# The first key projection between TensorE's turns, and three of eight one-hots multiplied on GpSimd

## What is computed

```python
xn = _layernorm(x, axis=-1)
# s: attention
q = (xn @ Wq + bq)                      # 8 heads of 128
k, v = split(xn @ Wkv + bkv)            # one head of 128 each
q, k = q + pe, k + pe                   # sinusoidal positions
probs = softmax(causal(q k^T / sqrt(128)))
s = (probs @ v) @ Wo
# g: experts, two of eight for each token
logits = xn @ router_w + router_b
gating = softmax(logits, the two largest kept)
y_e = relu(xn @ w1[e] + b1[e]) @ w2[e] + b2[e]
g = silu(sum_e gating[e] * y_e)
out = x + s * g
```

## Times and profile before

| | us |
|---|---|
| median of the runs before | 1032.6 (1032.31 to 1035.81) |
| the profiled execution | 1037.49, of which the span 1035.7 |
| TensorE busy in the span | 978.3 (94%) |
| VectorE busy | 875.0 (84%) |
| ScalarE busy | 646.0 (62%) |
| GpSimd busy | 338.6 (33%) |

### The profile page before, as it was taken

One profiled execution on the slowest core, in us unless ns is written; L12 is line 12 of the kernel. 1 busy time (PEld: TensorE's weight loads), 2 busy tenths in 40 slices (PEclk: granted clock), 3 DMA queues, 4 the chain that ended last, 5 costly groups with the idle time before them and its releaser, 6 DMA issues.

```text
span 1035.7 us, 25206 instructions
## 1 busy us (share of the span) xinstructions
PE 978.3 (94%) x8418; PEld 764.4 (74%) x8418; DVE 875.0 (84%) x1707; ACT 646.0 (62%) x1383; POOL 338.6 (33%) x342
## 2 busy tenths in 40 slices
PE   0799999999999899999998999999999999999997
PEld 0667888888889799976666666776766777777786
DVE  7899889887676455659999999999999999999972
ACT  4853333333333243438898988888888888888860
POOL 2017889999996300011010102121212121212111
PEclk9999999999999999999999999999999999999999
DMA  9866776766665523227999999999999999999993
GB/s 284 257 268 156 192 195 181 201 191 185 179 180 168 149 57 63 68 87 151 186 169 183 164 178 176 187 196 169 177 187 180 197 187 182 174 168 172 169 179 99
DMA packets 426749, 178.39 MB, mean 172 GB/s; under 512 B 362714, under 2 KB 416548, under 8 KB 425860
## 3 DMA queue, kind: packets, MB, share of 16 engines
q1 hardware_dynamic: 364644, 131.53, 63.1%
q10 hardware_dynamic: 55504, 27.55, 10.5%
q0 software_dynamic: 6480, 17.70, 7.2%
HBM read 54.42 MB, written 34.60 MB: 86 GB/s over the span
## 4 chain that ended last, share of the span: by engine, by line
PE 37%; DVE 13%; issue 2%; ACT 2%; DMA 1%; ACTq 0%; SPq 0%; DVEq 0%
PE b_psS L1411 11%; PE b_psO L1439 11%; PE b_psJ L1456 6%; PE b_psJ L1370 5%; DVE b_ph L1652 4%; DVE b_nmax L1614 4%; PE b_psS L1467 2%; PE b_psO L1442 1%; DMA b_pT<-b_ph 1%; DVE b_outs L1658 1%; ACT b_pr L1521 1%; DVE b_psJ L1622 1%; DVE b_Q L1636 1%; ACT b_ph L1551 1%; DVE b_f L1664 0%
## 5 line engine op out<-in xcount | busy, mean ns | idle before, releaser
L1054 PE MATMUL psU<-bxT,w_p 128*128 128x256 f16 (+1 forms) x1920 | 285.6, 261 | 2.8 <-issue 1.3
L1152 ACT ACTIVATE h<-psU,bias 128x256 f32<-128x256 f32 (+1 forms) x320 | 126.7, 447 | 243.9 <-PE psU L1054 211.4
L1063 PE MATMUL psY<-w_p,hp 128*128 x1704 | 272.3, 273 | 2.5 <-issue 1.4
L1521 ACT ACTIVATE b_pr<-b_psS,b_nmax 128x1024 f32<-128x1024 f32 (+7 forms) x256 | 188.2, 743 | 58.3 <-DVE b_nmax L1612 36.2
L1411 PE MATMUL b_psS<-b_kp,b_Q 128*128 128x512 f16 (+3 forms) x1152 | 215.1, 326 | 3.1 <-PEq L1251 1.5
L1439 PE MATMUL b_psO<-b_pT,b_vp 128*128 128x256 f16 x1536 | 204.4, 274 | 8.4 <-DMA b_pT<-b_ph 3.4
L1054 PEld LDWEIGHTS psU<-bxT,w_p 128*128 x1920 | 188.0, 98 | 22.3 <-issue 5.5
L1652 DVE SCALAR_TENSOR_TENSOR b_ph<-b_pr,b_rrec,b_ph 128x1024 f16<-128x1024 f32 (+7 forms) x256 | 199.3, 811 | 1.9 <-ACT b_ph L1551 1.9
L1551 ACT ACTIVATE b_ph<-b_pr,b_rrec 128x1024 f16<-128x1024 f32 (+7 forms) x256 | 187.9, 779 | 0.0
L1063 PEld LDWEIGHTS psY<-w_p,hp 128*128 128x128 f16 x1704 | 166.8, 98 | 22.5 <-issue 2.6
L1179 DVE CAST hp<-h 128x512 f16<-128x512 f32 (+1 forms) x160 | 92.9, 581 | 101.3 <-ACT h L1152 99.5
(11 more groups left out here) (198 smaller groups left out, 1072.2 us busy)
## 6 DMA issues: line engine op xcount, KB each, us to landing
wstage<-in_L_ffn_w SPq DMA_DIRECT2D x48, 256.0 KB
expert_rows<-rowx SPq DMA_DIRECT2D x65, 128.0 KB
expert_outputs<-y ACTq DMA_DIRECT2D x31, 256.0 KB
b_pT<-b_ph SPq DMA_TRANSPOSE x320
a_x_all<-in_L_attn_x SPq DMA_DIRECT2D x8, 512.0 KB, 7.4
a_w_raw<-in_L_ffn_w SPq DMA_DIRECT2D x4, 1024.0 KB, 9.7
xn_split<-a_xp SPq DMA_DIRECT2D x4, 1024.0 KB, 8.9
xn_turned<-a_xT SPq DMA_DIRECT2D x3, 1024.0 KB, 15.9
```

The source lines that it names most:

```text
L1054: mm = eng.matmul(psU[w % U][:, g % 2, 0:tiles * P].rearrange("p (t r) -> p t r", t=tiles), weight(n, a * W1 + c * H + g * P, P), bxT[n % ...
L1063: mm = eng.matmul(psY[n % 2][:, t, :], hp[n % 2][:, a, g, t * P:(t + 1) * P], weight(n, 2 * W1 + (2 * g + b) * D, D), start=(g == 0 and k ...
L1152: a = eng.activation(h32[w % 4][:, g, 0:rows], psU[w % U][:, g, 0:rows], ACT.Relu, bias=bias[:, ds(e * HT + 2 * q + g, 1)], scale=1.0 / WS)
L1521: a = eng.activation(pr[k % 3][:, o:o + w], psS[BUF[i]][:, :, :].rearrange("p a n -> p (a n)")[:, o:o + w], ACT.Exp, bias=nmax[:, at:at + ...
```

## The change

Four things are changed.

- `project(0)` moves from behind the logits to between the turns, behind turn(4) and its logits, and waits only for the first of the two weight splits (s_ks 1, L895). It goes to another bank (the second of the two psY banks), and the banks of r = 1 and 2 move too (`kq_bank`).
- The first later_kv (six steps) stands before `counts()`; 30 steps still stand between project(3) and the placing, so 20 rather than 26 remain behind it.
- With the banks moved, later_kv of h = 1, 2 and 3 wait for the copies of projections 0, 1 and 2; before it was h = 2, 3 and 4.
- For s = 1, 3 and 5 VectorE makes only the two comparisons, and GpSimd multiplies by the token numbers (`with_ids`), behind its two normalisations and ahead of its wait for the stored rows. `place(s)` waits for GpSimd's semaphore for those three.

```diff
+    kq_bank = [kv_bank[1], flat[0], flat[1], flat[3]]
+    s_plain, s_ids = sem("one_hot_plain"), sem("one_hot_with_ids")
+    IDS_BY_POOL = (1, 3, 5)
+    def with_ids(eng, s):
+        c = s * PER % NT
+        return eng.tensor_tensor(oh_q[:, s], oh_q[:, s], ids16[:, c:c + PER].unsqueeze(1).to_broadcast([P, UNITS, PER]), ALU.mult)
...
         def project(r):
-            eng.wait_ge(s_ks, 2)
+            eng.wait_ge(s_ks, 1 if r < 2 else 2)
...
-                    mm = eng.matmul(flat[r].rearrange("p (t n) -> p t n", n=P), w, xTb_next[:, 4 * j:4 * j + 4, 2 * b + c, :],
+                    mm = eng.matmul(kq_bank[r].rearrange("p (t n) -> p t n", n=P), w, xTb_next[:, 4 * j:4 * j + 4, 2 * b + c, :],
...
         def later_kv(h, k):
-            if k == 0 and 2 <= h < 5:
-                eng.wait_ge(s_kc, h - 1)
+            if k == 0 and 1 <= h < 4:
+                eng.wait_ge(s_kc, h)
...
         def place(s):
-            eng.wait_ge(s_oh, s + 1)
+            if s in IDS_BY_POOL:
+                eng.wait_ge(s_ids, before(s, IDS_BY_POOL))
+            else:
+                eng.wait_ge(s_oh, s + 1 - before(s, IDS_BY_POOL))
...
+            if e == 4:
+                project(0)
         logits(BY_DMA[-1])
         logits(TWOS - 2)
         logits(TWOS - 1)
-        for r in range(3):
+        for r in range(1, 3):
             project(r)
+        later = iter([(h, k) for h in range(len(KV)) for k in range(STEPS)])
+        for _ in range(STEPS):
+            later_kv(*next(later))
         eng.wait_ge(s_bz, 3)
         counts()
         project(3)
-        later = iter([(h, k) for h in range(len(KV)) for k in range(STEPS)])
         for _ in range(LEAD):
             later_kv(*next(later))
...
-            eng.activation(kq_f[:, r, :], flat[r], ACT.Copy, scale=SC / WS).then_inc(s_kc, 1)
+            eng.activation(kq_f[:, r, :], kq_bank[r], ACT.Copy, scale=SC / WS).then_inc(s_kc, 1)
...
         def one_hots(s):
+            if s in IDS_BY_POOL:
+                at = slice(s * PER, (s + 1) * PER)
+                step(eng.tensor_tensor(oh_r[:, s], lane16[:, :, :], r16[:, at].unsqueeze(1).to_broadcast([P, P, PER]), ALU.is_equal))
+                eng.tensor_tensor(oh_q[:, s], unit16[:, :, :], q16[:, at].unsqueeze(1).to_broadcast([P, UNITS, PER]),
+                                  ALU.is_equal).then_inc(s_plain, 1)
+                return
...
+        eng.wait_ge(s_tab, 4)
+        for s in IDS_BY_POOL:
+            eng.wait_ge(s_plain, before(s, IDS_BY_POOL))
+            with_ids(eng, s).then_inc(s_ids, 1)
         eng.wait_ge(xs_, 64)
```

More of the change, by code:

```diff
@@ L863, in one_hots @@
                                    ALU.is_equal))
-            c = s * PER % NT
-            eng.tensor_tensor(oh_q[:, s], oh_q[:, s], ids16[:, c:c + PER].unsqueeze(1).to_broadcast([P, UNITS, PER]),
-                              ALU.mult).then_inc(s_oh, 1)
+            with_ids(eng, s).then_inc(s_oh, 1)
         for g in range(4):
```

## The result

| | before | after |
|---|---|---|
| median, 21 runs of each | 1034.7 us | 1038.5 us |
| profiled execution (span) | 1037.5 (1035.7) | 1039.0 (1036.4) |
| ratio after to before | | 1.0038, 95% interval 1.0025 to 1.0051 |
| first expert matmul, in the profiled executions | 78.40 us | 81.44 us |

The changed kernel is 0.38% slower, about 3.9 us; the forecast was +3.2 us. The first expert matmul comes 3.04 us later. The sum was nearly met, but not by the terms that I had written down: some were too large, others were missing, and they nearly cancelled. The rows show how.

The account below looks back on a forecast made before the run. TensorE was taken to bound the kernel, setting placing's pace by 0.03 us over VectorE. The terms 0 + 0.4 + 0 + 2.76 gave +3.2 us, so 1032.6 + 3.2 = 1035.8 us for the median, range 1031.5 to 1038.8.

Parts of the forecast that it names:

- What bounds the front: Front, before the first expert matmul at 78.40 us: TensorE paces placing at 1.49 us a chunk, VectorE delivers in 1.46.
- Part 1: End of the front: six later_kv matmuls fewer behind place(7), 1.3 us less work, gains nothing; bounds 0 to -0.3 us.
- Part 2: Turning stage: project(0) between turns delays turn(5) by 0.97 us and turn(7) by 0.4; cost +0.4, bounds 0 to +1.0 us.
- rival C: Turning stage: project(0) brings TensorE to 2.4 GHz before the turns, -0.5 us; 1032.1 us without blocking or late place(1); chance 0.08.
- The wait of later_kv(1) for the copy of project(0): Behind the counts: TensorE waits 0.1 to 0.2 us for ScalarE's copy; cost 0, bounds 0 to +0.5 us.
- Part 3: Placing: three multiplications on GpSimd make TensorE wait and block VectorE's comparisons; 1.28 + 2 x 0.74 = +2.76 us.
- the hold T: Placing: time GpSimd's multiplication holds the shared port against VectorE; taken as 1.28 us, bounds 0.7 and 1.64.
- the formula 2.76 + 3 (T - 1.28): Placing: cost in us of the three GpSimd multiplications for a port hold of T, taken as 1.28 us.
- GpSimd's duration: Placing: a 568-element multiplication on GpSimd, scaled by length from L291, takes 1.28 us undisturbed.
- rival D: Placing: GpSimd's multiplication in rows of eight is much slower, over 1.95 us; slower by over 0.5%; chance 0.15.
- Rival B: Placing: GpSimd does not block VectorE's comparisons, only place(1) is 0.85 us late; total 1033.9 us; chance 0.32.
- The size: Whole kernel: 0 + 0.4 + 0 + 2.76 = +3.2 us, all before the first expert matmul, passed through one for one.

## Why the prediction was right, and where it was wrong

- **What bounds the front** (TensorE sets the pace of placing by 0.03 us, VectorE's relief is worth nothing): right. VectorE is idle for 2.10 us ahead of `who`; in the kernel before it was 0.40. The end follows the first expert matmul by the medians (+3.9 us), which is what the forecast took for granted, though not in the profiled pair.
- **Part 1, moving the six steps gains nothing**: right at full clock (1.21 us of idle time took their place without GpSimd's part), wrong in the changed kernel, where it saved about 0.7 us of what GpSimd's part costs, and 1.3 us where the clock fell sooner. I had taken the spacing of 0.216 us for given. One reading under it was wrong, too: the 0.4 us that a weight load waits for the gather in the earlier trace rows belong to the second tile, at 77.11; the first tile's load waited for no DMA. That the gather decides from 75.6 on was shown only by the run without GpSimd's part.
- **Part 2, +0.4 us**: the mechanism was right to 0.05 us as far as turn(7). The step that failed was the dismissal of rival C, "5 us of uninterrupted projections passed before the spacing halved, and project(0) is 2.6". In five of the eight executions with the moved projection the clock rose behind these 2.6 us, for two to four turns; in one of them, the run without steps between the chunks, it stayed up, and place(0) came at 59.09, near the 59.2 that rival C has. The first projection behind the logits starts, against 43.26 before, at 42.91 in the changed kernel; in the variants at 42.71, 43.23, 43.31 and 43.35, and at 43.59 and 43.60 (twice) where no turn ran faster. Those last are 0.34 late, near the forecast 0.4; the others are the same delay less what the clock gave back. At place(0) the eight stand between 0.60 us earlier and 0.53 later than the 59.69 of before.
- **The wait of later_kv(1) for the copy of project(0)**: forecast 0.1 to 0.2, 0.22 us in the trace, hidden as forecast.
- **Part 3, +2.76 us**: place(0) to place(7) grew by 3.04. The mechanism of the hold was right: GpSimd's multiplication counts from the end of VectorE's 1024-column comparison, and VectorE's next comparison stands still for it. The term that was mis-sized is the hold T: 1.28 us taken, 0.94 of standing still measured. With it the formula 2.76 + 3 (T - 1.28) gives 1.74, and the rows give 1.03 for the first hand-over and 0.38 for each of two pairs, together 1.8. My term was 1.0 us too large. The other 1.25 us is the clock, a term that the sum did not have at all: at 2.4 GHz place(7) would follow the 65.24 of place(3) by one pair of 3.36 and one of 2.98 us and stand at 71.58 instead of 72.83.
- **GpSimd's duration**: 1.44 and 1.51 us in the record, against 1.28 taken; but some 0.5 of it lies beside the comparison that is still running. The threshold of rival D (1.95) was not reached.
- **Rival B** (no blocking) falls by the 1.39 us comparisons. The rule of the Trainium skill that I cited, "SBUF — State Buffer", Who interferes with whom, is borne out for 16-bit one-hots as well. It lets the later instruction wait, and the trace agrees in both orders: the 1024-column comparison that had started first was not lengthened (0.69), and GpSimd's multiplication, started beside it, ended 0.98 to 1.01 us behind it in all 16 cases of the six kernels that have one.
- **The size**: +3.2 forecast, +3.9 measured with an interval of 2.6 to 5.3; 3.04 at the first expert matmul. The terms of the forecast, 3.16 before rounding, become the measured 3.04 like this: part 2 came out at -0.37 instead of +0.4 in this execution (-0.77), the hold was shorter (-0.97), the clock in placing was missing (+1.25), and so was what stands behind place(7), the later copy above all (+0.37). So the agreement owes much to luck: two errors of about 1 us stand against each other in placing, and two smaller ones outside it.

The 21 runs of the changed kernel agree with a part of the clock, but do not prove it: the fastest, 1034.2 us, is the one whose mean granted clock is 0.998; the other twenty lie at 0.985 to 0.996 and 1036.4 us or more, the one at 0.996 at 1038.0.

Open: which execution gets which timing of the clock, and whether the kernel before too has executions in which it falls in placing; no profile of one was taken. Its runs lie 8 us apart, and on the chip of the first experiments 7 of its 33 have a mean granted clock of 0.991 to 0.995 and a median of 1033.5 us, the other 26 at 0.997 to 0.999 a median of 1029.0; a mean doesn't say in which stage the clock was low. Open as well: what delays the copy of the second turned tile. No variant was faster than the kernel before.

## What to carry to other kernels

Before handing work from one engine to another, ask which engine sets the pace: here VectorE was relieved of 1.4 us that nobody waited for, at the price of a hand-over and of its own two-input instructions standing still beside GpSimd's. Work that fills TensorE between small matmuls may do a second job: in the executions profiled here the clock stayed up with it and fell without it, or behind a wait of under 1 us, and the wide matmuls behind took twice as long. A sum that comes out right is not yet a sum with the right terms: here four of them were off. In a sum over TensorE, write down for each stretch at which clock it is meant to run, and price it at the other.

## What the runs showed of the hardware that I had not expected

- Eight matmuls of 71 columns take 1.05 us at 2.4 GHz and 1.07 at 1.2; two of 512 columns 0.44 and 0.83. Only the wide ones pay for the low clock. Where TensorE had placing matmuls alone, the granted clock was 0.50 although it counts as busy for 1.8 of 2 us.
- After six 512-column matmuls amid turns the clock went to 2.4 GHz in five of eight executions and stayed at 1.2 in three; the same program, apart from what comes later. In four of the five it was back at 1.2 when the next projections began; in the fifth these took 1.46 us for six, so 2.4 GHz.
- A GpSimd instruction that reads two tiles and starts 0.2 us into a VectorE comparison of 0.69 us didn't lengthen that one, but held the next, 0.45 long, for 0.94 us. Its own end stood 0.98 to 1.01 us behind the first comparison's end in 16 of 16 cases, so its recorded 1.44 to 1.52 us seem to hold a wait.
